# A pass over eight graphs laid out anew: two woven parts and one more graph in flight

## The chip, the cores and the metric

The kernel runs on one core of one Trainium2 chip. The metric is the device time of one execution in microseconds, taken as the median over several runs. The profile is one further execution, recorded by the hardware profiler.

## What is computed

Eight graphs of 1024 nodes with 128 features each go through two layers, each a graph step and an expert step, every one on the normed residual stream and added to it.

```python
# layer 0, graph step: maximum over the first 25 neighbours by number
feats = jnp.where(valid[..., None], x[idx], -inf);  agg = feats.max(axis=2)
x = x + relu(concat([norm(x), agg]) @ W + b)
# layer 0, experts: 8 experts 128 -> 512 -> 128 (exact gelu), best two of each row
x = x + sum_e w_dense[:, e] * (gelu(norm(x) @ W1[e] + b1[e]) @ W2[e] + b2[e])
# layer 1, graph step: attention, 8 heads of 16, masked by the adjacency matrix
scores = where(adj > 0, q @ k.T / 4, -1e9);  x = x + softmax(scores) @ v @ Wo + bo
# layer 1, experts: 6 experts of three 128 x 128 layers, best two of each row
```

## The kernel before

**Order.** All engines walk one list of steps per pass, made in Python by `schedule` and `weave`. Each engine runs its own share of every step, in the list's order, and waits on semaphores where another engine or a DMA is needed. So an engine that waits holds up all that stands behind it in the list. DMAs are issued by SP (waits in order too) and by POOL, which issues the indirect ones.

**Pass.** A full pass does four things for four graphs: attention and second expert layer of graph b (flag `att`), first expert layer of b+1 (`unit`), graph step and routing of b+2 (`near`), loading and norming of b+3 (`load`). There are 11 passes, b = -3 to 7; five of them (0 to 4) are full.

**First stage** of a full pass. For 8 row tiles and 8 heads the step `s` computes 128 x 1024 scores (two bf16 matmuls, line 1521, into one of two PA banks) and VectorE adds the mask and takes the row maximum (line 1193). Woven in are the 23 blocks of the first expert layer: weights of a block loaded into one of three slots of `wbuf` (`wl`), up (line 1494), gelu on ScalarE (line 1323), down (line 1506). Two searches for neighbours (`find`) and their gathers (line 791) come between, too.

**Second stage.** Score products again in transposed form with mask and maximum inside the matmul (`st`, lines 1544 and 1547), exponential on ScalarE (line 1340), value products (`av`, line 1559), normalization (`fin`) and output projection (`proj`), 4 groups of 8 steps. Between them the other searches (`find` 2 to 7), gathers, slot maxima (`pmax`, lines 924 to 931), and at its start the fetch of the sorted expert rows (line 833) and their addition (`comb`, line 1041).

**Third stage.** Norm of the attention result (`lnv` 3, `ln` 3), transposes and router (`t1`, `r1`, `lg1`), then the 12 expert steps of the second expert layer (`u1`, `u2`, `y1`, `acc1`; lines 1601, 1608, 1616, 1091). Spread over them lies a chain: the graph step of b+2 (`gT`, `gnn`), norms, query, key and value of b+1 (`qT`, `qk`, `v`), routing of b+2 (`lg0`, `cha` 0, `rank`), dispatch of its rows (`disp`, line 823), norm of b+3. Query and key are split into three bf16 parts, stored to `parts_dram` and loaded as stacks into QS and KS.

## Time and profile before

| | us |
|---|---|
| median of 3 runs | 3739.25 (3731.97 to 3746.79) |
| profiled execution, its own time | 3723.76 |
| its span in the trace | 3721.9 |
| busy: TensorE, VectorE, ScalarE, GpSimd | 2235.3, 1751.5, 1199.4, 1129.4 |

PE is TensorE, DVE VectorE, ACT ScalarE, POOL GpSimd. Busy time is that in which an instruction of the engine runs; the profile gives idle time and what ended it apart. The granted clock is the share of TensorE's full clock; 0.50 is its lower level of 1.2 GHz, 1.00 the upper of 2.4 GHz. Time and span differ by 1.9 us, and the median stands 15.5 us above the profiled execution.

### The profile page before, as it was taken

How to read it: one execution, taken by the hardware profiler on the slowest of the kernel's cores; microseconds unless marked ns; L12 is line 12 of the kernel's file. 1: busy time of each engine (PE TensorE's matmuls, PEld its weight loads, DVE VectorE, ACT ScalarE, POOL GpSimd, SP SyncE). 2: the span in 40 equal slices, each digit the busy share in tenths (PEclk: the TensorE clock that was granted, in tenths of full speed). 3: DMA queues.
4: the chain of work that ended last, by engine and by line, in shares of the span. 5: the costliest groups of instructions: out<-in, count | busy, mean ns of one | idle time of the engine just before them, and what ended most of it. 6: DMA issues, size and time to landing. Idle time of an engine off the chain costs nothing.

```text
span 3721.9 us, 46486 instructions
## 1 busy us (share of the span) xinstructions
PE 2235.3 (60%) x14209; PEld 1335.1 (36%) x14209; DVE 1751.5 (47%) x5158; ACT 1199.4 (32%) x2272; POOL 1129.4 (30%) x1245
## 2 busy tenths in 40 slices
PE   0013214677656766677656766677567757896687
PEld 0013212443425333443335333443335433643044
DVE  4223116652565336652565336652575437614813
ACT  0002111235313442235322433235223532363044
POOL 3535451425132431425132431424133431010000
PEclk9986655789868877789868877788768977997588
DMA  4425635633356325633357225734257325502200
GB/s 94 49 31 141 102 67 107 165 88 48 54 141 158 45 37 104 165 92 48 53 142 160 42 38 108 162 96 47 38 144 175 47 35 114 168 9 43 59 1 7
DMA packets 190540, 318.62 MB, mean 86 GB/s; under 512 B 28832, under 2 KB 115101, under 8 KB 190237
## 3 DMA queue, kind: packets, MB, share of 16 engines
q1 hardware_dynamic: 149788, 221.18, 22.3%
q0 software_dynamic: 40448, 93.92, 18.8%
q8 instruction: 126, 2.06, 0.2%
q14 instruction: 178, 1.45, 0.1%
HBM read 271.67 MB, written 42.93 MB: 85 GB/s over the span
## 4 chain that ended last, share of the span: by engine, by line
issue 26%; PE 23%; DVE 22%; DMA 17%; POOL 4%; DVEq 4%; ACT 2%; SPq 2%; POOLq 1%; ACTq 0%
DMA wbuf<-in_L_ffn_W 9%; DVE parts L1193 7%; PE PH L1494 4%; DMA parts_dram<-parts 3%; PE PY L1506 3%; POOL G L791 3%; DMA xn<-in_x 3%; PE PA L1544 2%; PE PY L1559 2%; PE PA L1547 2%; PE PA L1521 2%; DVE G L924 2%; DVEq L845 1%; DVE xn L874 1%; POOL rows_cols L833 1%
## 5 line engine op out<-in xcount | busy, mean ns | idle before, releaser
L791 POOL DMA_INDIRECT G<-table,slot_idx x792 | 814.8, 1029 | 379.9 <-issue 379.9
L1193 DVE CUSTOM_DVE_ANT_0 parts<-PA,mask 128x1024 bf16<-128x1024 f32 x512 | 626.2, 1223 | 250.4 <-issue 250.4
L1340 ACT ACTIVATE HB<-PA 128x1024 f32<-128x1024 f32 x512 | 497.4, 1019 | 496.1 <-PE PA L1547 495.9
L1521 PE MATMUL PA<-KS,QS 96*128 96x512 bf16 x1024 | 405.1, 491 | 224.0 <-DVE MX L1193 174.3
L1544 PE MATMUL PA<-QS,KS 99*128 99x512 bf16 x1024 | 412.1, 402 | 85.4 <-ACT HB L1340 48.9
L631 POOL TENSOR_TENSOR pool_pad<-pool_pad 1x1 f32<-1x1 f32 x128 | 28.6, 224 | 1424.5 <-DVE expert L1032 553.3
L1547 PE MATMUL PA<-identb,mask 128*128 128x128 bf16 x4096 | 414.4, 225 | 0.0
L1494 PE MATMUL PH<-rows_cols,wbuf 128*128 128x128 f32 x1472 | 254.2, 328 | 242.3 <-DMA wbuf<-in_L_ffn_W 193.4
L1547 PEld LDWEIGHTS PA<-identb,mask 128*128 128x128 bf16 x4096 | 331.6, 101 | 135.3 <-issue 21.7
L1323 ACT ACTIVATE HB<-PH,wbuf 128x128 f32<-128x128 f32 x736 | 209.6, 368 | 453.9 <-PE PH L1494 451.1
L634 DVE MEMSET dve_pad<- 1x1 f32 x686 | 40.4, 59 | 635.2 <-DMA G<-table,slot_idx 362.9
L1494 PEld LDWEIGHTS PH<-rows_cols,wbuf 128*128 128x128 f32 x1472 | 224.8, 232 | 302.9 <-DMA wbuf<-in_L_ffn_W 200.8
L1559 PE MATMUL PY<-HB,VS 128*32 128x512 f32 x2048 | 282.0, 624 | 7.1 <-ACT HB L1340 7.1
L1521 PEld LDWEIGHTS PA<-KS,QS 96*128 96x128 bf16 x1024 | 89.9, 108 | 414.0 <-DVE MX L1193 347.8
L1506 PEld LDWEIGHTS PY<-wbuf,HB 128*128 128x128 f32 x1472 | 226.2, 224 | 26.0 <-issue 7.4
L1506 PE MATMUL PY<-wbuf,HB 128*128 128x128 f32 x1472 | 230.2, 308 | 0.7 <-ACT HB L1323 0.7
L1370 PE MATMUL PH<-ident,xn 128*128 128x128 f32 x320 | 64.0, 352 | 249.3 <-DVE xn L874 94.1
L1544 PEld LDWEIGHTS PA<-QS,KS 99*128 99x128 bf16 x1024 | 102.7, 100 | 262.1 <-ACT HB L1340 170.3
L1359 ACT ACTIVATE HB<-PH,bias_T 128x512 f32<-128x512 f32 x192 | 131.5, 686 | 193.7 <-PE PH L1601 130.6
L1263 ACT ACTIVATE edges<-adj_sb 128x1024 uint8<-128x1024 int32 x64 | 67.8, 1060 | 385.3 <-DMA adj_sb<-in_adj 385.1
L1388 PE MATMUL PH<-excess,ones 128*1 128x2 f32 x128 | 12.2, 165 | 271.6 <-ACT excess L1266 231.5
L1616 PE MATMUL PY<-ew_sb,HB 128*128 128x128 f32 x768 | 122.5, 311 | 66.0 <-DVE mask L1091 62.3
(197 smaller groups left out, 2808.0 us busy)
## 6 DMA issues: line engine op xcount, KB each, us to landing
wbuf<-in_L_ffn_W SPq DMA_DIRECT2D x184, 514.0 KB, 4.9
adjm<-in_adj SPq DMA_DIRECT2D x64, 512.0 KB
adj_sb<-in_adj POOLq DMA_DIRECT2D x48, 512.0 KB, 3.9
G<-table,slot_idx POOLq DMA_INDIRECT x792
parts_dram<-parts SPq DMA_DIRECT2D x16, 768.0 KB, 6.8
QS<-parts_dram SPq DMA_DIRECT2D x48, 256.0 KB, 8.4
KS<-parts_dram SPq DMA_DIRECT2D x48, 256.0 KB, 8.4
rows_cols<-sorted_x SPq DMA_DIRECT2D x40, 256.0 KB, 4.7
```

The lines of the kernel that those rows point to most:

```text
L791: pool.indirect_dma_start(G[:, t % 2, s, :], None, table, bass.IndirectOffsetOnAxis(slot_idx[:, t, s:s + 1], axis=0), bounds_check=ROWS - ...
L1193: ins = dve.tensor_tensor_reduce(out=junk, in0=psum(ps, step)[:, :], in1=mask[:, t, :], scale=1.0, scalar=LOWEST, op0=ALU.add, op1=ALU.max ...
L1323: ins = act.activation(HB[:, 1, j % 2, c * P:(c + 1) * P], psum(ps, step)[:, c * P:(c + 1) * P], ACT.Gelu, bias=wbuf[:, j % WRING, 2 * HID ...
L1340: act.activation(HB[:, kc % 2, 2 * pr:2 * pr + 2, :], psum(ps, key)[:, :].rearrange("p (h q) -> p h q", h=2), ACT.Exp, scale=float(D) ** - ...
L1359: act.activation(HB[:, 0, k + j % 2, :], psum(ps, step)[:, :], ACT.Relu, bias=bias_T[:, col + e:col + e + 1]).then_inc(*emptied(ps, step))
L1494: ins = pe.matmul(psum(ps, step)[:, c * P:(c + 1) * P], wbuf[:, j % WRING, c * P:(c + 1) * P], cols_x[:, g % 2, q * P:(q + 1) * P], start= ...
L1506: ins = pe.matmul(psum(ps, ("y", g))[:, q * C:(q + 1) * C], HB[:, 1, j % 2, c * P:(c + 1) * P], wbuf[:, j % WRING, HID0 + c * C:HID0 + (c ...
L1521: ins = pe.matmul(psum(ps, step)[:, half[hf]], QS[0:SROWS, h, t * P:(t + 1) * P], KS[0:SROWS, h, half[hf]], start=True, stop=True)
L1544: pe.matmul(o, KS[0:SROWS + PARTS, h, kc * P:(kc + 1) * P], QS[0:SROWS + PARTS, h, half[qh]], start=True, stop=False)
L1547: ins = pe.matmul(o[:, qt * P:(qt + 1) * P], mask[:, qh * HTILES + qt, kc * P:(kc + 1) * P], identb[:, :], start=False, stop=(qt == HTILES ...
L1559: ins = pe.matmul(psum(ps, key)[32 * hh:32 * hh + 32, :], VS[:, kc, (D + 1) * (g * GH + hh):(D + 1) * (g * GH + hh) + 32], HB[:, kc % 2, h ...
L1616: ins = pe.matmul(psum(ps, step)[:, tt * C:(tt + 1) * C], HB[:, 0, 2 + j % 2, tt * P:(tt + 1) * P], ew_sb[:, 2, e, :], start=True, stop=True)
```

## The change

The pass becomes two parts, A and B, each an order merged from streams by planned times (`merge`): the step with the earliest planned time goes next, unless a step that it must follow, or the one that frees its PSUM bank, isn't placed yet. The planned times only order the list; nothing waits for them.

Part A (planned times 0 to 130): the second expert layer of graph b-1 with its norm and router; score maxima of b; expert blocks of b+1; `pmax` 3 to 7 of b+2 with the fetches of tiles 4 to 7. Part B (0 to 118): value products of b; graph step, norm, routing and dispatch of b+2; fetch and joining of expert rows, norm, query and key of b+1; load, norm, table, all eight searches, four fetches and three `pmax` of b+3. Then `stack`, `v`, the last `fin` and `proj`.

A fifth flag, `late`, stands for the second expert layer of b-1. There are 12 passes, b = -3 to 8; four of them (1 to 4) are full. The stage of the last expert layer runs alone in the last pass.

Further: weights of the blocks have six slots (four in `wbuf`, one in HB, one in `parts`) in place of three; their biases come no longer with the weights but are worked out by VectorE after `rank` (`block_b1`). Gathered slots beyond the eighth go to one shared buffer `G_more`, so their fetch waits for `pmax` t-1. The stacks of QS and KS are loaded after the last `st` in a step of their own. All adjacency loads come from SP. `gT`, `gnn`, `r1`, `lg0`, `lg1`, `rank`, `chb` and `chc` take banks PH; `y1` takes PA. Four residual buffers stand where there were two and a piece of the mask; norms have their own small tiles.

```diff
-FINDS_EARLY = 10
 BLOCKS = 2 * TILES + E0 - 1
 PER_GROUP = 4
 GROUPS = (BLOCKS + PER_GROUP - 1) // PER_GROUP
-WRING = 3
-BLOCKS_FROM = 22.0
-WCOLS = 2 * HID0 + HC
+WOWN = 4
+WRING = WOWN + 2
+WCOLS = 2 * HID0
+FETCHED = 4
+POOLED = FETCHED - 1
...
+def merge(streams, held):
+    s, done = [], set()
+    heads = [0] * len(streams)
+    known = {step for stream in streams for _, step, _ in stream}
+    while any(h < len(stream) for h, stream in zip(heads, streams)):
+        best = None
+        for n, stream in enumerate(streams):
+            if heads[n] == len(stream):
+                continue
+            when, step, after = stream[heads[n]]
+            if any(a in known and a not in done for a in after) or best and best[0] <= when:
+                continue
+            taken = {name: list(held[name]) for name in held}
+            for name, key, _ in signals(step):
+                if name in BANKS:
+                    if len(taken[name]) >= BANKS[name]:
+                        before = taken[name][-BANKS[name]]
+                        if before in known and before not in done and before != step:
+                            break
+                    taken[name].append(empties(step, key))
+            else:
+                best = when, n, step, taken
+        _, n, step, taken = best
+        heads[n] += 1
+        done.add(step)
+        for name in held:
+            held[name][:] = taken[name][-4:]
         s.append(step)
+    return s
+def over(begin, end, steps):
+    return [(begin + (end - begin) * n / len(steps), step, after) for n, (step, after) in enumerate(steps)]
+def chained(times, steps):
+    return [(t, step, (steps[n - 1],) if n else ()) for n, (t, step) in enumerate(zip(times, steps))]
...
+def schedule(late, att, unit, near, load):
+    n1 = len(ORDER1)
+    streams = []
+    tail = []
+    if late:
+        tail += [("x2",)]
+    if att or unit:
+        tail += [("take",)]
+    if near:
+        tail += [("load_res",)]
+    streams.append([(0.0, k, ()) for k in tail])
+    if late:
+        streams.append(chained((0, 4, 11, 15, 20, 20.1, 28, 31),
+                               [("lnv", 3), ("ln", 3), ("t1",), ("r1",), ("lg1",), ("cha", 1), ("chb", 1), ("chc", 1)]))
+        experts = []
+        for k in range(n1 + 2):
+            if k < n1:
+                experts.append((("u1", k), (("t1",),)))
+            if 1 <= k <= n1:
+                experts.append((("u2", k - 1), (("u1", k - 1),)))
+            if k >= 2:
+                experts.append((("y1", k - 2), (("u2", k - 2),)))
+                experts.append((("acc1", k - 2), (("y1", k - 2), ("chc", 1))))
+        streams.append(over(33, 128, experts) + [(128.0, ("store",), ())])
+    if near:
+        streams.append([(15.0 * (t - POOLED), ("pmax", t), (("fetch", t),)) for t in range(POOLED, TILES)])
+        streams.append([(15.0 * (t - POOLED) - 14.0, ("fetch", t), (("pmax", t - 1),)) for t in range(FETCHED, TILES)])
     if att:
+        scores = []
         for t in range(TILES):
+            scores.append((("mask", t), (("load_mask", t),)))
+            for h in range(HEADS):
+                scores.append((("s", t, h), ()))
+                if h == 2 and t + 1 < TILES:
+                    scores.append((("load_mask", t + 1), (("mask", t),)))
+        streams.append(over(9, 130, scores))
     if unit:
+        first = [("xs", 0), ("xs", 1)] + [("wl", j) for j in range(WRING)]
+        blocks = [(("xT", 0), (("xs", 0),))]
         for j in range(BLOCKS + 1):
             if j < BLOCKS:
                 if j % PER_GROUP == 2 and j // PER_GROUP + 1 < GROUPS:
+                    g = j // PER_GROUP + 1
+                    blocks.append((("xT", g), (("xs", g),)))
+                    if g + 1 < GROUPS:
+                        blocks.append((("xs", g + 1), ()))
+                blocks.append((("up", j), ()))
             if j > 0:
+                blocks.append((("dn", j - 1), ()))
                 if j - 1 + WRING < BLOCKS:
+                    blocks.append((("wl", j - 1 + WRING), ()))
                 g, last = group_of(j - 1)
                 if last:
+                    blocks += [(("yc", g), ()), (("yst", g), ())]
+        streams.append([(0.0, k, ()) for k in first] + over(7, 116, blocks))
+    held = {"A": [], "H": [], "Y": []}
+    s = merge([k for k in streams if k], held)
+    streams = [[(0.0, ("shift",), ())]]
     if att:
+        streams.append(chained((0.1, 1.5), [("mparts",), ("mT",)]))
+        values = []
+        groups = [(qh, g) for qh in range(2) for g in range(2)]
         for n, (qh, g) in enumerate(groups):
             for kc in range(TILES):
+                values.append((("st", qh, g, kc), (("mT",),)))
                 if kc == 1 and n > 0:
+                    values.append((("fin", *groups[n - 1]), ()))
                 if kc == 3 and n == 2:
+                    values.append((("proj", 0), ()))
                 if kc > 0:
+                    values.append((("av", qh, g, kc - 1), ()))
+            values.append((("av", qh, g, TILES - 1), ()))
+        streams.append(over(5, 118, values))
+    if near:
+        graphs = chained((0.2, 5, 5.1, 12, 17, 23, 27, 27.1),
+                         [("gT",), ("gnn",), ("gnn_add",), ("lnv", 1), ("ln", 1), ("t0",), ("lg0",), ("cha", 0)])
+        if not unit:
+            graphs.insert(1, (0.3, ("bias",), ()))
+        graphs += [(47.0, ("rank",), (("comb",),)), (54.0, ("disp",), ()),
+                   (56.0, ("chb", 0), (("comb",),)), (57.0, ("chc", 0), ())]
+        streams.append(graphs)
+    if unit:
+        streams.append([(2.0, ("fetch_y",), ())])
+        streams.append([(36.0, ("comb",), (("fetch_y",),)), (38.0, ("lnv", 2), ()), (43.0, ("ln", 2), ()),
+                        (50.0, ("qT",), (("lg0",),)), (57.0, ("qk", 0), ()), (67.0, ("qk", 1), ()),
+                        (75.0, ("next_mask",), ())])
+    if load:
+        streams.append([(7.0, ("load_x",), (("gT",),)), (19.0, ("lnv", 0), ()), (23.0, ("ln", 0), ()),
+                        (28.0, ("store_x",), ())])
+        finds = [(8.0, ("load_adj", 0), ()), (8.0, ("load_adj", 1), ()),
+                 (9.0, ("deg", 0), (("gT",),)), (11.0, ("class", 0), ())]
+        for t in range(TILES):
+            when = 14.0 + 12.5 * t
+            finds.append((when, ("find", t), ()))
+            if t + 2 < TILES:
+                finds.append((when + 2, ("load_adj", t + 2), ()))
+            if t + 1 < TILES:
+                finds.append((when + 5, ("deg", t + 1), ()))
+                finds.append((when + 9, ("class", t + 1), ()))
+        streams.append(finds)
+        streams.append([(30.0 + 15.0 * t, ("fetch", t), (("find", t), ("store_x",), ("pmax", t - 1)))
+                        for t in range(FETCHED)])
+        streams.append([(82.0 + 17.0 * t, ("pmax", t), (("fetch", t),)) for t in range(POOLED)])
+    s += merge([k for k in streams if k], held)
+    if unit:
+        s += [("stack",), ("v",)]
     if att:
...
+    if k == "fetch":
+        t = step[1]
+        return [(f"gat{t % 2}", step, 16 * SLOTS)]
...
-        return Y(*step)
+        return A(*step)
...
-        wbuf = sb("wbuf", [P, WRING, WCOLS])
+        wbuf = sb("wbuf", [P, WOWN, WCOLS])
...
-        G = sb("G", [P, 2, SLOTS, C])
+        G = sb("G", [P, 2, CLASS_SLOTS[0], C])
+        G_more = sb("G_more", [P, SLOTS - CLASS_SLOTS[0], C])
...
+        XF = XT2
         rest = tmp
-        CT = tmp
-        ctxn = xn[:, 0:HTILES, :]
+        col_sums = WT
+        wslots = [wbuf[:, i, :] for i in range(WOWN)]
...
-            parts_of = (g >= 0, 0 <= g + 1 < GRAPHS, 0 <= g + 2 < GRAPHS, g + 3 < GRAPHS)
-            if g > 0 and all(parts_of):
+        for g in range(-3, GRAPHS + 1):
+            parts_of = tuple(0 <= g + ahead < GRAPHS for ahead in (-1, 0, 1, 2, 3))
+            if g > 1 and all(parts_of):
                 continue
             passes.append((g, Pass(state, *parts_of)))
-            loops = GRAPHS - 3 if all(parts_of) else 1
...
-                        for j, k in enumerate(which):
+                    elif kind == "stack":
+                        sp.wait_ge(*at(ps, turn, "pd", ("qk", 1)))
+                        if ps.att:
+                            sp.sem_inc(s_slot, 1)
+                            sp.wait_ge(*is_full(ps, turn, ("st", 1, 1, TILES - 1, 1)))
+                        stacks = [(i, stack, j, k) for i, (stack, which) in enumerate(((QS, QPART), (KS, KPART)))
+                                  for j, k in enumerate(which)]
+                        for n, (i, stack, j, k) in enumerate(stacks):
+                            if ps.att and n == len(stacks) - 1:
+                                sp.wait_ge(*is_full(ps, turn, ("av", 1, 1)))
                             sp.dma_start(stack[D * j:D * j + D, :, :],
...
+                    for s in range(few - 2, few):
+                        fetch(s)
+                    if t >= 1:
+                        pool.wait_ge(*at(ps, turn, "aggr", ("pmax", t - 1)))
+                        held_by(pool, pool_pad, True)
...
+                settle(dve.tensor_scalar(expert_f[:, :], expert_f[:, :], float(E0 - 1), None, ALU.min))
+                dve.tensor_copy(expert[:, :], expert_f[0:1, :]).then_inc(S["pos"], 1)
+                settle(dve.tensor_tensor(passed[:, :, :], expert_f[:, :].unsqueeze(2).to_broadcast([P, BLOCKS, EP]),
+                                         eidx[:, 0:1, :].to_broadcast([P, BLOCKS, EP]), ALU.is_equal))
+                for lo, hi in ((0, BLOCKS // 2), (BLOCKS // 2, BLOCKS)):
+                    n = hi - lo
+                    spare = tmp[:, 0:n * HC * EP].rearrange("p (j c e) -> p j c e", c=HC, e=EP)
+                    settle(dve.tensor_tensor(spare, passed[:, lo:hi, :].unsqueeze(2).to_broadcast([P, n, HC, EP]),
+                                             b1_sb[:, :, :].unsqueeze(1).to_broadcast([P, n, HC, EP]), ALU.mult))
+                    settle(dve.tensor_reduce(out=block_b1[:, lo:hi, :], in_=spare, axis=AX.X, op=ALU.add))
...
+                        if j == 0:
+                            act.wait_ge(*at(ps, turn, "bb"))
...
```

## Rows read from the trace of the kernel before

**Rows 1.** The page: the span, and the busy time of each engine.
```profile
span 3721.9 us, 46486 instructions
...
PE 2235.3 (60%) x14209; PEld 1335.1 (36%) x14209; DVE 1751.5 (47%) x5158; ACT 1199.4 (32%) x2272; POOL 1129.4 (30%) x1245
```

**Rows 2.** Line 1193 in five windows: duration min/median/max, first and last start.
```profile
L1193 DVE CUSTOM_DVE_ANT_0 parts<-PA,mask x64: 1218/1224/1226, 636.5 to 788.2; 128x1024 bf16<-128x1024 f32 x64
...
L1193 DVE CUSTOM_DVE_ANT_0 parts<-PA,mask x64: 1218/1224/1226, 1475.0 to 1627.9; 128x1024 bf16<-128x1024 f32 x64
...
L1193 DVE CUSTOM_DVE_ANT_0 parts<-PA,mask x64: 1218/1223/1225, 2737.0 to 2885.2; 128x1024 bf16<-128x1024 f32 x64
...
L1193 DVE CUSTOM_DVE_ANT_0 parts<-PA,mask x64: 1218/1224/1226, 3132.5 to 3238.2; 128x1024 bf16<-128x1024 f32 x64
...
L1193 DVE CUSTOM_DVE_ANT_0 parts<-PA,mask x64: 1223/1224/1225, 3453.2 to 3547.5; 128x1024 bf16<-128x1024 f32 x64
```

**Rows 3.** Windows: length; busy of PE, PEld, DVE, ACT, POOL; clock; DMA share; GB/s.
```profile
1475.00:1629.00 154.00, 102.70 (x522) 70.43 (x521) 102.25 (x224) 39.89 (x123) 43.43 (x46) 0.75 0.59 147
1629.00:1786.00 157.00, 107.84 (x949) 56.54 (x949) 50.29 (x129) 73.94 (x102) 77.96 (x87) 0.83 0.29 44
1786.00:1895.00 109.00, 70.10 (x306) 42.78 (x306) 64.98 (x290) 35.57 (x59) 17.23 (x18) 0.80 0.46 90
3132.00:3240.00 108.00, 88.23 (x499) 58.38 (x500) 87.70 (x204) 32.72 (x100) 7.21 (x8) 0.84 0.60 181
3453.00:3549.00 96.00, 64.16 (x124) 8.16 (x124) 87.80 (x203) 0.00 (x0) 0.00 (x0) 0.50 0.12 39
3549.00:3662.00 113.00, 100.40 (x939) 52.21 (x939) 9.95 (x25) 64.60 (x67) 0.00 (x0) 0.95 0.01 2
3662.00:3722.00 60.00, 42.01 (x177) 24.95 (x177) 25.68 (x121) 20.99 (x32) 0.00 (x0) 0.81 0.03 10
```

**Rows 4.** The same for two short windows.
```profile
1490.00:1510.00 20.00, 6.21 (x12) 0.79 (x12) 17.50 (x33) 0.00 (x0) 0.18 (x1) 0.50 0.33 110
1730.00:1750.00 20.00, 18.20 (x181) 9.55 (x179) 5.79 (x15) 14.13 (x22) 9.76 (x12) 1.00 0.28 54
```

**Rows 5.** Lines, 1475 to 1629 us: count, busy, mean ns, idle before and releaser.
```profile
L791 POOL DMA_INDIRECT G<-table,slot_idx x41 | 41.7, 1017 | 13.3 <-issue 13.3
L1494 PE MATMUL PH<-rows_cols,wbuf 128*128 128x128 f32 x184 | 34.8, 350 | 28.5 <-DMA wbuf<-in_L_ffn_W 27.4 <-ACT rows_cols L1317 0.9
```

**Rows 6.** Waits, 1629 to 1786 us: total, times, longest.
```profile
PE PH L1569 <- DVE tmp L1222: 29.0, 3, 19.0
...
DVE res_n L1041 <- issue: 19.9, 1, 19.9
...
DVE dve_pad L634 <- DMA G<-table,slot_idx: 18.0, 2, 12.9
```

**Rows 7.** Lines of the whole span, gathers, scatters, slot maxima and table loads.
```profile
L791 POOL DMA_INDIRECT G<-table,slot_idx x792 | 814.8, 1029 | 379.9 <-issue 379.9
...
L833 POOL DMA_INDIRECT rows_cols<-sorted_y,place x128 | 127.8, 998 | 56.8 <-issue 56.8
L823 POOL DMA_INDIRECT sorted_x<-xn,place x128 | 125.2, 978 | 49.5 <-issue 49.5
...
L924 DVE TENSOR_TENSOR G<-G 128x256 f32<-128x256 f32 (+5 forms) x154 | 110.9, 720 | 59.7 <-issue 53.0
...
L1278 ACT ACT_TABLE_LOAD x24 | 30.8, 1283 | 23.9 <-DVE sd L859 23.5
...
L1107 DVE TENSOR_TENSOR parts<-tmp,parts 128x512 bf16<-128x512 f32 x32 | 22.1, 692 | 2.4
```

**Rows 8.** DMA issues: count, size of one, median us to landing.
```profile
wbuf<-in_L_ffn_W SPq DMA_DIRECT2D x184, 514.0 KB, 4.9
...
QS<-parts_dram SPq DMA_DIRECT2D x48, 256.0 KB, 8.4
```

**Rows 9.** Line 791 in 1629 to 1786 us, as in group 5.
```profile
L791 POOL DMA_INDIRECT G<-table,slot_idx x55 | 56.8, 1033 | 32.6 <-issue 32.6
```

384 lines of the change are left out of this document (132 added, 252 removed).

## Prediction

> **What bounds the kernel now.** I read the share of busy time first: TensorE works 2235 of 3722 us, VectorE 1752 [rows 1]. No engine fills the span, so the limits change from stage to stage or come from waits. The score line at different places shows the beat: first scores at 636.5 us, then from 1475.0 to 2737.0 three passes, 420.7 us each; the pass from 3132.5 to 3453.2 takes 321 us, and 269 us follow to the end [rows 1, 2]. The windows split a full pass into 154 us of scores with blocks and two searches, 157 us of values with six searches and 109 us of second expert layer with the chain [rows 3]. In the first DVE is busy 102 of 154 us with PE at 103, in the second PE 108 of 157 with DVE at 50, in the third PE 70 and DVE 65 of 109. Each stage leaves room on both.
>
> The last passes show the same stages with less beside them, and these are the best prices in the trace. Scores alone: 96 us, limited by DVE, which is busy 87.8; a stretch full of scores has DVE at 17.5 of 20 us, its practical top, and PE at 6 with the clock at 0.50 [rows 3, 4]. Scores and blocks without searches and gathers: 108 us, with PE 88 and DMA at 181 GB/s. Values alone: 113 us, PE busy 100 at clock 0.95. Second expert layer alone, from the norm to the store: 60 us, PE 42, DVE 26 [rows 3].
>
> **Part A** puts scores, blocks, second expert layer and five slot maxima together. On DVE: scores with masks 96 us; expert layer 25.7 busy, at 17.5 of 20 some 29 us; slot maxima 110.9 us at their main line over 64 tiles [rows 7], 1.7 us each, with final step and waits between dependent steps about 3, so five cost 15; copies of the residual 2. Sum 142 us. On PE: 88 for scores and blocks and 42 for the expert layer make 130 busy; the fullest stretch has 18.2 of 20 [rows 4], so 143 us. DMA: 181 GB/s over 108 us are 19.5 MB; the gathers of four tiles add 38 x 64 KB, result and residual 1 MB, together 23 MB or 127 us at that rate. Three loads near 140 us have to interlock. The stage with scores and blocks took 108 us against 96 on DVE, a factor of 1.13. The one with two searches took 154 against 96 and two searches of about 11 us, a factor of 1.31; there the blocks waited 27.4 us for weights [rows 5], with three slots, and gathers shared the DMA engines. Six slots should take much of that wait away, but four tiles of gathers remain. I take 1.18, so 167 us, between 142 and 1.31 x 142 = 186.
>
> At the seam the stacks come late. They are 12 loads of 256 KB, one landing after 8.4 us [rows 8]; 3.1 MB at 181 GB/s are 17 us from the last `st`. The last `av`, `fin`, `proj` and the copies hide about 12, and SP stands at the stack and then at `load_res`, so the first six weight loads follow behind. I add 5 us to each A, between 0 and 15: A = 172.
>
> **Part B** puts values and the chain together. On PE: 100 busy for the values; the third stage's 70 less the layer's 42 leave 28 for the chain; 128 busy, at the 100.4 of 113 that the values reach alone 144 us. If the 49 us of PE's idle time in the present value stage stayed, it would be 177. Part of that idle time had a cause that the plan addresses: PE waited 29.0 us in three `fin` steps for the copy by DVE, which itself stood 19.9 us for the joined expert rows and 18.0 for gathers [rows 6]. `comb` is now planned at 36, after 20 us of fetch. On DVE the searches and the rest are the pass's 217 us of busy time less about 128 in A, so some 90, or 103 at its top density; not the limit. The new block biases are four passes over 384 elements of a row; the nearest row is 128 x 512 at 0.69 us [rows 7], so at most 2.8 us, and `rank`'s other readers go first.
>
> POOL decides more. A gather costs 1.51 us with its idle time (814.8 + 379.9 over 792), a fetch of expert rows 1.44 and a scatter 1.36 [rows 7]. In B it does 16 fetches (23 us), then tile 0 once the new table is stored (about 35), 25 gathers (38 us, to 73), the dispatch (22, to 95), tile 1 (16 gathers, to 119), tile 2 (about 10, to 134). 41 gathers for two tiles are read from the first stage [rows 5]; the other six tiles share 58. Then `pmax` 2 can run at about 140 where 116 is planned, and DVE, PE and the rest behind it in the list wait for it. About 15 us of values and the 12 us of `fin` and `proj` follow. B = 165, between 144 and 190.
>
> A full pass is thus 337 us in place of 421. ScalarE is at 74 of 157 us in the value stage and 40 of 154 in the first, so it hides its new work. A norm's square root between exponentials or gelus costs table loads; they are 1.28 us each and there are 24 at the norm line now, three per full pass [rows 7]. I count four more per pass, 5 us, hidden. The Trainium skill, in "ScalarE: Activation LUTs", What ACT_TABLE_LOAD costs, speaks against such mixing: every switch of set costs the load and a drain, some 2.66 us, and calls should be batched by set. By it the four would cost 11 us per pass; as an estimate 80 us over the kernel if nothing hid them. The rows agree on the 1283 ns of the load; the drain they do not show.
>
> **The sum.** Before its first scores the kernel still has to gather for two graphs and run the blocks of one. The two woven parts bring these together, but one chain on POOL remains; I take 615 us for 636.5, between 560 and 670. b = 0 has no second expert layer: on DVE 113 us, at 1.18 with the seam 140, and 165: 305. Four full passes: 4 x 337 = 1348. b = 5, without searches: 172 + 150. b = 6, without graph work: 160 + 130. b = 7: scores and expert layer, 125 us on DVE, so 137, and 113 for values. b = 8: 60. Together 615 + 305 + 1348 + 322 + 290 + 250 + 60 = 3190; 1.9 us lie around the span and the median stood 15.5 above the profiled execution: **3207 us**, with 3100 to 3320 if A and B stay within 10 us each of these values.
>
> **The rivals.** *POOL and DMA keep the beat* (0.27). With A and B shorter, gathers and weight loads meet more often. If tiles 0 to 3 take more gathers, or `G_more` with its wait for `pmax` t-1 stops POOL at tile 1, B becomes 185; if gathers slow the weights as in the first stage now, A 186. The pass takes 371 us, and six such passes give 3207 + 6 x 34 = 3410. For it speak the 154 us against 108 [rows 3]. A gather took 1.34 us with its idle time in the first stage, 1.63 in the second [rows 5, 9], though the latter waits for tiles between. The Trainium skill, "SBUF — State Buffer", says that a two-port VectorE operation locks GpSimd out of writing descriptors; that would be one cause. A busier DVE would then lengthen the gathers, and the rows so far do not show it, since the stage with more DVE work has the cheaper ones.
>
> *Everything fits* (0.08). The clock rises with fuller PE, A comes to 150 and B to 150: 3207 - 6 x 37 = 2990.
>
> *The order stalls the engines, slower than before* (0.12). Engines run one written order, by planned times that sum to 248 us where I expect 337. B has about 20 places at which PE waits for DVE or ScalarE in a chain step (`fin`, `proj`, `t0`, `lg0`, `rank`, `qT`, `class` and so on), while DVE may itself wait for a gather. Three such places cost 29.0 us before, about 10 each [rows 6]. If all 20 cost 5 us more than I allow, a pass grows by 100 us and the time is 3207 + 6 x 100 = 3810. The change is slower from 90 us per pass, 4.5 us a place. Against it: the steps of a stream stand several values apart, and values alone leave ScalarE and DVE enough time to answer.
>
> *Most of the gain is lost* (0.05): the same with half the price, or weaving that hides little, 3500 to 3720.
>
> **How the numbers follow.** The forecast has 0.48. The range is 3030 to 3500: it takes the forecast's own, POOL's case, and the upper part of the good one. About 0.5% is what a measurement of this kernel can tell from no change. Faster by more 0.87, within it 0.02, slower by more 0.11.
>
> **What would show it.** First scores from pass to pass every 337 us; A near 172 with DVE over 75% busy and a mean clock above the 0.75 of the first stage; little waiting of PE for wbuf; in B POOL in work nearly throughout until `pmax` 2, and DVE's waits before slot maxima 1 and 2. Wrong would be: B over 200 with PE waiting at chain steps; weight waits as long as now; a long pause between the last `st` and the first scores.

## The result and the profile after

The changed kernel takes 3597.73 us (3594.47 to 3601.75), the kernel before on the same chip 3735.61 (3727.08 to 3746.79): a ratio of 0.963, interval 0.960 to 0.966. The direction was as forecast. The size was not: 138 us gained where 3207 us stood for 532, and the time lies above the upper end of the range, 3500. The profiled execution took 3601.75 us.

The head of the page of after, its span and its busy times, answers to [rows 1]:

```profile
span 3599.6 us, 46254 instructions
...
PE 2146.0 (60%) x14209; PEld 1346.9 (37%) x14209; DVE 1776.8 (49%) x5239; ACT 1226.7 (34%) x2295; POOL 1106.3 (31%) x1215
```

TensorE has 89 us less work, VectorE 25 us more, and the span is 122 us shorter. TensorE still fills 60% of it, VectorE 49% instead of 47: no engine is near to filling it.

The score line in six windows answers to [rows 2]. It is line 1221 now; each line gives the first and the last of 64 maxima of one graph (its custom instruction alone; the shortest, the median and the longest in ns ahead of the times):

```profile
L1221 DVE CUSTOM_DVE_ANT_0 parts<-PA,mask x64: 1218/1224/1226, 720.8 to 851.3; 128x1024 bf16<-128x1024 f32 x64
...
L1221 DVE CUSTOM_DVE_ANT_0 parts<-PA,mask x64: 1218/1220/1225, 1460.3 to 1626.2; 128x1024 bf16<-128x1024 f32 x64
...
L1221 DVE CUSTOM_DVE_ANT_0 parts<-PA,mask x64: 1218/1220/1225, 1848.1 to 2017.5; 128x1024 bf16<-128x1024 f32 x64
...
L1221 DVE CUSTOM_DVE_ANT_0 parts<-PA,mask x64: 1218/1220/1225, 2640.9 to 2810.3; 128x1024 bf16<-128x1024 f32 x64
...
L1221 DVE CUSTOM_DVE_ANT_0 parts<-PA,mask x64: 1216/1220/1225, 2977.5 to 3127.5; 128x1024 bf16<-128x1024 f32 x64
...
L1221 DVE CUSTOM_DVE_ANT_0 parts<-PA,mask x64: 1214/1220/1226, 3279.1 to 3421.0; 128x1024 bf16<-128x1024 f32 x64
```

First scores at 720.8 instead of 636.5 us: the beginning became longer, not shorter. Then 1460.3 to 1848.1, one full pass, is 388 us instead of 420.7, and 1848.1 to 2640.9, two more, are 396 each. The passes after that take 337 and 302 us, as the work beside the scores goes away.

For the windows I cut each pass at two steps that are easy to find in the trace: A begins where the residual of the graph is kept (step `x2`) and ends where the maxima leave for the value stage (step `mparts`); B goes from there to the next `x2`. The columns are window, length, busy us of PE, weight load, DVE, ACT and POOL with their counts, granted clock, DMA share, GB/s. The rows are A and B of b = 2, A and B of b = 7, and the last expert layer alone; they answer to [rows 3]:

```profile
1444.20:1628.00 183.80, 137.37 (x708) 96.94 (x708) 121.08 (x348) 57.00 (x140) 49.71 (x54) 0.82 0.47 125
1628.00:1831.70 203.70, 130.11 (x1070) 72.81 (x1068) 97.94 (x301) 97.18 (x148) 88.35 (x93) 0.80 0.46 80
3261.00:3423.00 162.00, 95.29 (x305) 42.22 (x305) 112.24 (x322) 20.99 (x32) 0.00 (x0) 0.74 0.18 38
3423.00:3534.00 111.00, 100.06 (x939) 51.96 (x939) 8.53 (x22) 64.43 (x67) 0.00 (x0) 0.96 0.01 2
3534.00:3600.00 66.00, 44.07 (x178) 26.19 (x177) 27.29 (x124) 21.09 (x33) 0.00 (x0) 0.79 0.03 9
```

| part | predicted | measured |
|---|---|---|
| up to the first scores | 615 | 721 |
| b = 0, A and B | 140 + 165 = 305 | 133 + 199 = 332 |
| A of b = 1 to 4 | 172 | 187, 185, 188, 219 |
| B of b = 1 to 4 | 165 | 204, 203, 187, 181 |
| b = 5 | 172 + 150 | 206 + 141 |
| b = 6 | 160 + 130 | 176 + 131 |
| b = 7 | 137 + 113 | 163 + 113 |
| b = 8 | 60 | 64 |

The differences are 106 + 27 + 206 (four full passes) + 25 + 17 + 25 + 4 = 410 us, the whole distance from 3190 to the span of 3600. Added up by kind of part, the beginning is 106 us too long, the B's are 140 (34 in b = 0, 39, 38, 22 and 16 in the full passes) and the A's 160 (91 in the full passes, half of it in b = 4, and 34, 16 and 26 in b = 5 to 7).

**B of b = 2.** Its waits, 1628 to 1832 us (engine, operand and line, what ended the wait, us in total, times, longest):

```profile
POOL pool_pad L636 <- DMA table<-xn: 43.9, 1, 43.9
DVE dve_pad L639 <- DMA G_more<-table,slot_idx: 42.0, 2, 31.4
...
PE PH L1604 <- DVE rows_y L1255: 35.1, 1, 35.1
```

The work itself is where I put it: PE is busy 130 of 204 us where I summed 128, DVE 98 where I took some 90. But DVE waits 42 us for gathered slots beyond the eighth, and PE 35 us in the last `fin`, which waits for DVE. The time line of the end of tiles 1 and 2 shows how (start in us, length, engine, instruction; in brackets the idle time ahead of it and what ended it):

```profile
1774.95 0.06 DVE L639 MEMSET dve_pad<- 1x1 f32 x1 [10.62 <-DMA G_more<-table,slot_idx]
...
1775.37 0.18 POOL L636 TENSOR_TENSOR pool_pad<-pool_pad 1x1 f32<-1x1 f32 x1 [5.15 <-issue]
1775.93 1.23 DVE L941 TENSOR_TENSOR G<-G,G_more 128x1024 f32<-128x1024 f32 x1 [0.92 <-issue]
...
1776.96 1.08 POOL L803 DMA_INDIRECT G<-table,slot_idx  x1 [1.40 <-issue]
...
1779.15 0.06 DVE L956 MEMSET dve_pad<- 1x1 f32 x1 [0.29 <-issue]
...
1787.73 0.18 POOL L636 TENSOR_TENSOR pool_pad<-pool_pad 1x1 f32<-1x1 f32 x1
1799.83 1.01 POOL L803 DMA_INDIRECT G_more<-table,slot_idx  x1 [11.91 <-issue]
...
1808.95 0.99 POOL L803 DMA_INDIRECT G_more<-table,slot_idx  x1 [0.30 <-issue]
...
1814.94 0.06 DVE L639 MEMSET dve_pad<- 1x1 f32 x1 [31.37 <-DMA G_more<-table,slot_idx]
```

DVE gets tile 1's extra slots at 1774.95 and is done with them at 1779.15 (line 956 is the signal). GpSimd issues eight gathers of tile 2 up to 1787.7, stands 11.9 us, issues eight more into `G_more` from 1799.8 to 1809, and they have landed at 1814.94. That is 187 us into B where I put slot maximum 2 at about 140. The value products had been through at 1783.1, 155 us into B, and 17 us follow on slot maximum 2 to the end of B. At tile 1 the buffer was in use: GpSimd went on right after slot maximum 0. In B of b = 3 and 4 tile 2 has eight slots and tile 3 sixteen; these B's are shorter, and the A's behind them begin with a longer wait.

**A of b = 2.** Its longest waits of PE (1444 to 1628 us):

```profile
PE PA L1556 <- DVE res_f L1115: 20.1, 9, 3.6
...
PE PH L1519 <- DMA rows_cols<-sorted_x: 14.0, 1, 14.0
...
PE PH L1529 <- DMA wbuf<-in_L_ffn_W: 2.5, 2, 1.5
```

Waits for block weights are down to 2.5 us from 27.4 [rows 5]. Three steps take their place. The blocks' rows, dispatched at the end of B, arrive 14 us late. The second expert layer's product `y1` now uses bank PA, which the scores use, so that PE waits 20.1 us for the addition by DVE (line 1115, `acc1`), nine times. And the scores begin 17 us after the start of `x2`.

### The profile page after: what moved, and what is told of

It is laid out like the page before. It is cut to its first block, busy times and chain, and to the rows that moved or that the text cites. A ratio compares the mean times of both kernels' runs of the same rounds, so it can differ in the third digit from the quotient of the medians.

```text
span 3599.6 us, 46254 instructions
## 1 busy us (share of the span) xinstructions
PE 2146.0 (60%) x14209; PEld 1346.9 (37%) x14209; DVE 1776.8 (49%) x5239; ACT 1226.7 (34%) x2295; POOL 1106.3 (31%) x1215
## 4 chain that ended last, share of the span: by engine, by line
issue 35%; DVE 27%; PE 26%; DVEq 5%; ACT 4%; DMA 2%; SPq 1%; ACTq 0%
DVE parts L1221 7%; PE PA L1579 4%; PE PA L1582 4%; PE PY L1594 4%; ACT HB L1375 2%; PE PH L1529 2%; DVEq L861 2%; DVE res_f L1115 2%; PE PA L1556 2%; PE PY L1541 2%; DVE score L909 1%; DVE top L913 1%; PE PH L1636 1%; DMA rows_cols<-sorted_x 1%; DVE st L870 1%
## 5 line engine op out<-in xcount | busy, mean ns | idle before, releaser
L803 POOL DMA_INDIRECT G<-table,slot_idx x512 | 526.7, 1029 | 270.2 <-issue 270.2
L1556 PE MATMUL PA<-KS,QS 96*128 96x512 bf16 x1024 | 356.2, 441 | 261.5 <-DVE res_f L1115 141.5
L803 POOL DMA_INDIRECT G_more<-table,slot_idx x280 | 287.1, 1025 | 173.4 <-issue 173.4
L1358 ACT ACTIVATE HB<-PH,block_b 128x128 f32<-128x128 f32 x736 | 209.6, 368 | 353.7 <-PE PH L1529 353.6
L1519 PE MATMUL PH<-ident,rows_cols 128*128 128x128 f32 x184 | 35.4, 323 | 264.7 <-DMA rows_cols<-sorted_x 264.7
L1529 PE MATMUL PH<-rows_cols,wbuf 128*128 128x128 f32 x1024 | 166.8, 317 | 28.1 <-DMA wbuf<-in_L_ffn_W 20.0
L1529 PEld LDWEIGHTS PH<-rows_cols,wbuf 128*128 128x128 f32 x1024 | 158.5, 230 | 61.7 <-issue 29.0
L1285 ACT ACTIVATE XT<-PH 128x512 f32<-128x512 f32 x96 | 54.5, 597 | 358.6 <-PE PH L1405 358.3
L839 POOL DMA_INDIRECT sorted_x<-xn,place x128 | 130.6, 1020 | 65.2 <-issue 65.2
L1541 PEld LDWEIGHTS PY<-wbuf,HB 128*128 128x128 f32 x1024 | 142.3, 206 | 21.7 <-issue 10.9
```

What stands on the lines that cost most here:

```text
L803: pool.indirect_dma_start(G[:, t % 2, s, :] if s < few else G_more[:, s - few, :], None, table, bass.IndirectOffsetOnAxis(slot_idx[:, t, s ...
L839: pool.indirect_dma_start(sorted_x, bass.IndirectOffsetOnAxis(place[:, j:j + 1], axis=0), xn[:, j % TILES, :], None, bounds_check=BLOCKS * ...
L1358: ins = act.activation(HB[:, 1, j % 2, c * P:(c + 1) * P], psum(ps, step)[:, c * P:(c + 1) * P], ACT.Gelu, bias=block_b1[:, j, c:c + 1])
L1529: ins = pe.matmul(psum(ps, step)[:, c * P:(c + 1) * P], wslots[j % WRING][:, c * P:(c + 1) * P], cols_x[:, g % 2, q * P:(q + 1) * P], star ...
L1541: ins = pe.matmul(psum(ps, ("y", g))[:, q * C:(q + 1) * C], HB[:, 1, j % 2, c * P:(c + 1) * P], wslots[j % WRING][:, HID0 + c * C:HID0 + ( ...
L1556: ins = pe.matmul(psum(ps, step)[:, half[hf]], QS[0:SROWS, h, t * P:(t + 1) * P], KS[0:SROWS, h, half[hf]], start=True, stop=True)
```

## The experiments

Five chips were used, called here the first to the fifth. Each kernel is compared with the kernel before on its own chip. Lengths of parts are compared across the first two, where the kernel before takes 3732 and 3724 us; the change itself was not run on the second. On the first chip ran the change itself again, eight slots, the split stacks and three weight slots:

> The changed kernel itself, unaltered, as a measure for the variants on the chip on which they run. On the first chip its ratio to the kernel before was 0.963. If the other chip only stretches all work alike, the ratio is 0.96 again; if it adds waits of its own to the longer chains of the two parts, it is nearer to 1, about 0.98.

Measured: 3593.04 us against 3731.71, ratio 0.9625 (0.9587 to 0.9662).

### Eight slots only

```diff
-                which = pool.value_load(degree_class[0:1, t:t + 1], ...)
...
-                with pool.If(which < 1):
-                    fetch(few - 2, ...); fetch(few - 1, ...)
+                fetch(few - 2, ...); fetch(few - 1, ...)
+                return
```

> Gathers and slot maxima are cut to eight slots for every tile (tiles with more neighbours are left incomplete): 64 gathers per graph for 97, none into G_more, so no wait for the buffer that tiles share. Theory 1, gathers through one queue and one shared buffer set the end of B: VectorE's two waits in B of 10.6 and 31.4 us fall under 5 us each, B from 204 to about 170, and the first three passes, which are nothing but this chain, shrink by 50 us or more: about 0.065 of the time, ratio to before near 0.90. Theory 2, chain steps of TensorE set B: B stays over 190, the ratio at 0.95 or above.

Measured: 3218.43 us, ratio 0.862 (0.8585 to 0.8654). The score line and the windows of A and B of b = 2:

```profile
L1213 DVE CUSTOM_DVE_ANT_0 parts<-PA,mask x64: 1220/1225/1226, 534.8 to 659.7; 128x1024 bf16<-128x1024 f32 x64
...
L1213 DVE CUSTOM_DVE_ANT_0 parts<-PA,mask x64: 1219/1220/1225, 1206.1 to 1363.2; 128x1024 bf16<-128x1024 f32 x64
...
L1213 DVE CUSTOM_DVE_ANT_0 parts<-PA,mask x64: 1219/1220/1226, 1560.4 to 1717.5; 128x1024 bf16<-128x1024 f32 x64
```

```profile
1186.20:1365.00 178.80, 130.95 (x708) 91.62 (x709) 121.28 (x350) 57.04 (x140) 40.34 (x45) 0.84 0.51 131
1365.00:1540.00 175.00, 127.58 (x1070) 71.22 (x1068) 92.48 (x298) 97.21 (x148) 61.81 (x67) 0.85 0.34 78
```

The first scores come at 535 us and B falls from 203 to 175; A is 179 instead of 185. GpSimd is busy 62 us in B instead of 88. So the slots beyond the eighth cost 375 us of the kernel; I had expected a ratio of 0.90, not 0.862. Of these 186 lie before the first scores and 43 in b = 0, since 721 and 332 us became 535 and 289. In the full passes 140 us go, 85 in the B's and 41 in A of b = 4, and what is left over my 165 is 9 to 12 us in three B's and nothing in the fourth. That the whole kernel comes to my 3207 plus 11 is chance in part: 80 us less than I had before the first scores stand against 67 more in the four full passes. The edit takes the slots' transfers, DVE's maxima over them and the shared buffer away together; two of the next runs take it apart in part.

### Two buffers for the extra slots

```diff
-        G_more = sb("G_more", [P, SLOTS - CLASS_SLOTS[0], C])
+        G_more = sb("G_more", [P, 2, SLOTS - CLASS_SLOTS[0], C])
...
-                    if t >= 1:
-                        pool.wait_ge(*at(ps, turn, "aggr", ("pmax", t - 1)))
-                        held_by(pool, pool_pad, True)
```

The room comes from the ring of weights (`WOWN` 1 instead of 4). In the order a fetch no longer follows slot maximum t-1 but t-2, and by that the dispatch comes to stand behind tile 1's gathers instead of ahead of them.

> All 97 gathers stay, but the slots beyond the eighth get a buffer for even and one for odd tiles, so that they wait for the slot maximum of tile t-2 and not of tile t-1. The room comes from the weights: one slot of their own in place of four, three in all, which the run with three slots showed to cost nothing. It tells the two halves of the gather theory apart, the number of gathers (33 more than in the run with eight slots, 1.5 us each, 50 us per graph) and the wait for the shared buffer. If the shared buffer is the cost: VectorE's wait of 31.4 us at the end of B falls under 8 us, B from 204 to about 178, the first three passes lose 60 us or more; together near 3400, ratio 0.91. If the number of gathers is the cost: B stays over 195, ratio 0.955 or above.

Measured on the second chip: 3507.24 us against 3724.39, ratio 0.9423 (0.9399 to 0.9447); the change stood at 0.9625 on the first. B of b = 2 falls from 203 to 192, first scores from 721 to 702, A is 188. Tile 2 on GpSimd now:

```profile
1733.62 1.04 POOL L803 DMA_INDIRECT G<-table,slot_idx  x1 [1.42 <-issue]
...
1743.56 1.00 POOL L803 DMA_INDIRECT G<-table,slot_idx  x1 [0.30 <-issue]
...
1744.86 0.99 POOL L803 DMA_INDIRECT G_more<-table,slot_idx  x1 [0.30 <-issue]
...
1753.96 0.99 POOL L803 DMA_INDIRECT G_more<-table,slot_idx  x1 [0.30 <-issue]
1754.97 0.18 POOL L636 TENSOR_TENSOR pool_pad<-pool_pad 1x1 f32<-1x1 f32 x1
...
1767.46 0.18 POOL L636 TENSOR_TENSOR pool_pad<-pool_pad 1x1 f32<-1x1 f32 x1 [12.31 <-issue]
```

Sixteen gathers in a row take 21 us, where the change needed 33, and the pause is gone. At tile 2 it had not been the buffer that was in use: in after slot maximum 1 had ended at 1779.15, before the pause began. What stands there is `held_by` (line 636), an addition of one element with a drain behind it. Where this pair follows at once on gathers, GpSimd's next instruction comes late, here 12.31 us after sixteen gathers, in after 5.15 and 11.91 us. DVE still waits for tile 2:

```profile
DVE dve_pad L639 <- DMA G_more<-table,slot_idx: 28.9, 1, 28.9
```

The B's of the full passes are 10, 11, 10 and 14 us shorter. In b = 2 only 5 of the 11 us are tile 2's own: from its first gather until DVE has it pass 33 us instead of 38, though the issues take 12 less. Without the pause the last gather lands 12.8 us after its issue (1753.96 to 1766.71) instead of 6 (1808.95 to 1814.94), so more than half of the pause was time that tile 2's transfers needed anyway. The other 6 us are a start 142 instead of 149 us into B, by the shorter wait at tile 1 and the moved dispatch, which no run takes apart. The ratio lies between my two cases, 0.91 and 0.955. The larger rest is the work that stands ahead of slot maximum 2 in GpSimd's queue, from which the next run moves the slot maximum away.

### Fewer tiles fetched in B

```diff
-FETCHED = 4
+FETCHED = 3
```

> FETCHED 3 on the chip of the unaltered kernel: three fetches and two slot maxima in B, five and six in A. With the run of eight slots, B without the chain is 175 us. Only the wait for tile 2, 31.4 us, leaves B, A takes up a slot maximum and may wait for tile 2's gathers at its start. Gather theory: B 178, A up by 5 to 15, ratio to before 0.93 to 0.945. If the wait only moves over the seam: 0.96.

Measured: 3534.68 us, ratio 0.9474 (0.9444 to 0.9504), on the second chip too. The fetch of tile 3 and slot maximum 2 are now in A. B of b = 2 is 175 (minus 28), the same as with eight slots. But A grows from 185 to 208, and the scores of its graph start 27 us after `x2` instead of 17. Of the 28 us that the order takes out of B, 23 come back behind the seam. The rest of the gain is in the first scores (706) and in b = 0 (297 instead of 332).

### `y1` in the banks PH

```diff
-        return A(*step)
+        return H(*step)
```

> y1 in a bank of PH, on the chip of the unaltered kernel. If sharing PA is the cost: TensorE's wait of 20 us for VectorE's adding of experts goes and A falls by 10 to 20 us, ratio 0.925 to 0.945. If VectorE sets A, or the PH banks stop the blocks: 0.955 to 0.97.

Measured on the second chip: 3545.25 us, ratio 0.9518 (0.9495 to 0.954). A of b = 2 is 180 instead of 185. In b = 7, where only scores and the expert layer stand, the score line runs

```profile
L1221 DVE CUSTOM_DVE_ANT_0 parts<-PA,mask x64: 1214/1224/1225, 3235.6 to 3359.2; 128x1024 bf16<-128x1024 f32 x64
```

from 3235.6 to 3359.2 us: 124 us against 142 in after (3279.1 to 3421.0), and that is the 125 us that I had worked out for VectorE alone. So the shared bank lengthens A by 5 to 12 us in the full passes and by 18 in b = 7, 68 us over b = 1 to 7, which the prediction had left out. The last expert layer alone gets 7 us longer with it (71 instead of 64). The gain is less than the 0.925 to 0.945 that I had expected.

### The stacks in two steps

```diff
-                            sp.dma_start(stack[D * j:D * j + D, :, :],
-                                         parts_v[i, k, :, :, :])...
+                            sp.dma_start(stack[D * j:D * j + D, lo:lo + GH, :],
+                                         parts_v[i, k, :, lo:lo + GH, :])...
+        streams.append([(91.0, ("stack0",), (("qk", 1), ("st", 1, 0, TILES - 1)))])
```

Four of the eight heads' stacks are loaded as soon as the last `st` of these heads is done.

> Heads 0 to 3 of QS and KS, which the last group of value products no longer reads, are loaded after the last st of group (1,0), some 30 us earlier; heads 4 to 7 stay where they are. Theory, the seam: in part A the first scores wait for the stacks (16.9 us from the kept residual to the first score in the changed kernel, 19.7 us of TensorE's wait in the last scores), and the weights and sorted rows queue behind 3.1 MB. With half of it gone the first rows land 8 us earlier: 6 to 10 us in each of seven seams, 40 to 70 us, 0.015 of the time. Rival: the loads meet gathers of tiles 1 and 2, on which VectorE waits at that time, and B grows by as much: no difference over 0.5%.

Measured on the first chip: 3547.76 us, ratio 0.9516 (0.9479 to 0.9554), 45 us less than the change on this chip. In b = 7 the first scores stand 8 us after `x2` instead of 19:

```profile
L1223 DVE CUSTOM_DVE_ANT_0 parts<-PA,mask x64: 1219/1224/1225, 3225.0 to 3363.4; 128x1024 bf16<-128x1024 f32 x64
```

A falls by 15 us each in b = 6 and 7, whose seams were 24 and 19 us. In the full passes the seam gives 1 us: something else is late there, among it the dispatched rows. The rest of the 45 us is 1 to 7 us in many parts, the most of it before the first scores and in A of b = 0; two profiles of the change differ by up to 5 us in a part.

### Three weight slots

```diff
-WRING = WOWN + 2
+WRING = 3
```

> Three weight slots in place of six, everything else as in the changed kernel. TensorE waits 2.5 us for weights in a part A of the changed kernel, 27.4 us in the first stage of the kernel before. Theory, the deeper ring is what took that wait away: it returns in part, 10 to 25 us in each of seven passes with blocks, 70 to 170 us, ratio to before 0.98 to 1.01. Rival, the looser order of A gives each block so much time that three slots are enough: ratio within 0.5% of the unaltered kernel.

Measured on the first chip: 3584.50 us, ratio 0.9604 (0.9565 to 0.9644), not to be told from the change. PE's wait for weights in A of b = 2 is 1.8 us against 2.5. What took the 27.4 us of [rows 5] away is therefore not the number of slots. The blocks are spread over 184 us in place of 154 with their weights ahead of them in the order; which of these does it was not tried.

### Together

Two buffers, `y1` in PH and the split stacks in one kernel:

> The three changes together: own buffers for the slots of even and odd tiles with three weight slots, stacks loaded in two halves, y1 in PH. If the three act on different places (end of B, seam, inside of A), the gains add: from 0.9625 some 0.05, 0.011 and 0.025, ratio near 0.875, 3270 us. If one wait hides behind another, it comes to 0.90 to 0.92.

Measured on the second chip: 3426.05 us against 3724.39, ratio 0.9203 (0.9188 to 0.9218): faster than both kernels, than the change by 4.4% by the two ratios. The three edits alone gave 0.020, 0.011 and 0.011 against the change, together 0.042, and this is the 0.042 between 0.9625 and 0.9203: the gains add. I had expected 0.875 in that case because I had set the single gains too high. The windows of A and B of b = 2:

```profile
1389.50:1564.00 174.50, 132.64 (x712) 92.74 (x712) 122.34 (x350) 57.77 (x142) 46.27 (x53) 0.85 0.49 130
1564.00:1755.30 191.30, 129.03 (x1064) 72.03 (x1064) 98.17 (x302) 96.47 (x147) 91.34 (x93) 0.83 0.46 86
```

A fell from 185 to 175 and B from 203 to 191; first scores at 700.

Then with three tiles fetched in B (best2), with a late dispatch on top (best3), and the eight-slot kernel with `y1` in PH and the split stacks (eight_all), on the third chip:

> The three changes (two buffers for slots beyond the eighth, split stacks, y1 in PH) with FETCHED 3, so that tile 2's slot maximum and tile 3's fetch move into part A. If the order of the queue is the cost, B loses the 29.9 us wait and A gains under 12: ratio 0.89 to 0.90, from 0.9203. If GpSimd's work as such is the cost, the wait shows up in A: 0.915 to 0.925.

> As the one before, and the dispatch behind the third fetch in place of behind the first. With own buffers nothing else stops GpSimd at tile 1, so its gathers and tile 2's end 30 us earlier, and the dispatch has the rest of B for itself. Order theory: a further 5 to 15 us per pass, ratio 0.875 to 0.89. Rival: sorted rows are then late for the blocks of the next part A, and the ratio is that of the run before or worse.

> Eight slots only (tiles with more neighbours are left incomplete), one buffer as in the changed kernel, six weight slots, stacks split, y1 in PH. B stays at 175 less 5. A was 179 with eight slots: if shared banks and seam are what lies above my 142 us of VectorE work, A falls to 155 and the ratio from 0.862 to about 0.82. If the mutual waits of the woven order are the cost, A stays over 168, ratio 0.84 to 0.85.

The kernel before takes 3939.81 us there, these 3774.70 (ratio 0.9565, 0.9527 to 0.9603), 3780.26 (0.9586, 0.9548 to 0.9624) and 3390.45 (0.860, 0.8559 to 0.864). With three tiles fetched in B the late dispatch changes nothing that can be measured. In eight_all A of the full passes is 174 to 180 us with a seam of 14, and the A's of b = 1 to 7 are together 87 us shorter than with eight slots alone on the first chip, 30 of them in b = 7. So the two other edits do show. But B of the full passes takes 213 to 219 where it took 164 to 177, and the ratio is the one that eight slots alone had. These B's belong to the chip, as the last runs show for the change; eight slots alone did not run here.

### The other chips

Four single edits ran on the fourth chip. The first of them:

```diff
-        graphs += [..., (54.0, ("disp",), ()), ...]
+        streams.append([(117.5, ("disp",), (("rank",), ("fetch", FETCHED - 1)))])
```

> Only the place of the dispatch in the order changes: in part B it comes behind the fourth fetch (planned 117.5) in place of behind the first (54). Theory 1, the one queue of GpSimd sets the end of B: in the profile of the changed kernel VectorE stands 10.6 and 31.4 us before the slot maxima of tiles 1 and 2, while the dispatch with its wait took GpSimd from 1707 to 1743 us. Without it ahead, the gathers of tiles 1 and 2 end 36 us earlier, VectorE's waits for them fall from 42 to under 12 us per pass, and B from 204 to about 172; in the six passes that fetch, about 180 us: 3420 us. Theory 2, B is limited by the chain steps that TensorE waits for and the gather wait only lies in front of them: B stays over 195 and the time over 3560. Theory 3, the dispatch then ends so late that part A waits for its sorted rows: B falls, A grows by as much.

> FETCHED 3 in place of 4: part B does three fetches and two slot maxima, part A five fetches and six slot maxima. Theory 1 (GpSimd's queue sets the end of B): the wait of 31.4 us for tile 2 leaves B, B falls from 204 to about 175, A grows by 3 us of slot maximum and by what it waits for tile 2's gathers at its start, at most 10: the time is about 3460. Theory 2 (chain steps limit B): B over 195, time over 3560. A rival on A's side: the wait of VectorE only moves behind the seam, A grows by as much as B loses, 3590.

> FETCHED 2: part B does two fetches and one slot maximum, part A six fetches and seven slot maxima. Theory 1: both waits, 42 us, leave B; B is near 165 as its TensorE work of 130 us at 0.9 busy allows with its start; A grows by two slot maxima of 3 us, and its gathers (56 of 97) meet the weight loads: A 187 to 200. The time is about 3430 if A hides them, 3520 if GpSimd's 85 us of gathers in A stop VectorE. Theory 2: over 3560.

> The last matmuls of an expert of layer 1 (y1) take a bank of PH in place of PA. In part A of the changed kernel TensorE waits 20.1 us for VectorE's adding of experts (line 1115), which frees the PA bank that the next score needs. Theory 1, sharing PA is the cost: the wait goes, part A falls from 185 by 10 to 20 us, the seven parts A with this layer give 70 to 140 us: 3460 to 3530. Rival: the PH banks, now held until VectorE has added, stop the blocks' up products; part A stays or grows, 3600 to 3700. Second rival: VectorE and its many waits for the next score set A whatever bank is used: within 1% of 3598.

| edit | us | ratio | A (seam) of b = 2 | B of b = 2 | first scores |
|---|---|---|---|---|---|
| dispatch behind the fetches | 3900.08 | 0.9899 (0.9866 to 0.9932) | 213 (33) | 233 | 727 |
| three tiles in B | 3854.49 | 0.9774 (0.9729 to 0.9819) | 201 (22) | 242 | 706 |
| two tiles in B | 3873.75 | 0.9826 (0.9785 to 0.9866) | 210 (14) | 242 | 673 |
| `y1` in PH | 3834.48 | 0.9735 (0.9692 to 0.9777) | 182 (18) | 257 | 716 |

The kernel before took 3947.70 us here. Against the kernel with `y1` moved the late dispatch has a B 24 us shorter and an A 31 us longer, 15 of them in the seam; some 5 to 12 of the 31 are the gain of the moved `y1`. It is the same trade over the seam. It could not bring tiles 1 and 2 forward by the 36 us that I expected, because the shared buffer holds tile 1: with the dispatch gone GpSimd stands there in B of b = 2 until slot maximum 0,

```profile
POOL pool_pad L637 <- DVE dve_pad L957: 60.0, 1, 60.0
```

which DVE reaches in its own order. Two tiles move the first scores 33 us forward against three, but A of b = 0 to 2 is 20, 13 and 9 us longer, and the kernel is 19 us slower.

These B are 30 to 54 us longer than the change's on the first chip. Three runs on the fifth chip, where the kernel before takes 3902.03 us, ask whether that belongs to the edits:

> The changed kernel unaltered. On the chip with 3730 us: 0.9625. On the other: FETCHED 3 alone gave 0.977 and y1 in PH alone 0.974 there, so 0.985 to 1.0 if these two gain as much there as on the first chip.

> best1 again, as a measure. On the chip with 3730 us for the kernel before: 0.92. On the chip with 3940 us, where B's chain steps wait more: 0.95 to 0.97, if the added waits fall into the chains that part B holds.

> Two buffers, split stacks, y1 in PH and FETCHED 3, beside best1 on the same chip. If the order of GpSimd's queue is the cost of the 29.9 us wait: 0.02 to 0.03 below best1. If GpSimd's work as such is the cost, the same as best1 within 0.005.

Measured: 3872.06 us (0.9918, 0.9888 to 0.9948), 3753.56 (0.9647, 0.9587 to 0.9708), 3742.82 (0.9598, 0.9541 to 0.9654). The unchanged change has A of 192 and 188 us for b = 1 and 2, about as before, and B of 252 and 253 instead of 204 and 203. It belongs to the chip. Three tiles or four cannot be told apart in the combined kernel, since the intervals overlap. Waits of the change here over the whole trace, which have no counterpart on the first chip:

```profile
ACT HB L1375 <- remote: 205.2, 52, 13.8
...
DVE WT L1095 <- remote: 89.7, 6, 17.7
...
ACT ed L1345 <- remote: 74.8, 5, 15.9
```

B of b = 2 on the fifth chip as a window, and two waits of GpSimd in it:

```profile
1732.40:1985.30 252.90, 143.81 (x1072) 77.48 (x1072) 98.19 (x301) 99.33 (x150) 84.67 (x93) 0.74 0.36 64
...
POOL pool_pad L636 <- DVE expert L1048: 32.8, 1, 32.8
POOL pool_pad L636 <- DVE dve_pad L956: 28.7, 1, 28.7
```

ACT stands 408 us in 87 such places and DVE 208 us in 26; "remote" says that the profile finds no instruction that ended just then. In 108 of the 113 the engine waits for a PSUM bank that PE fills: the signal comes later than the profile's end of the matmul. PE is busy 144 us in B of b = 2 (130 on the first chip), at a clock of 0.74 (0.80). GpSimd, too, waits for others there: 33 us for the routing (`rank`) and 29 for slot maximum 0, against 5.6 and 1.4 on the first chip. So on this chip its own queue is not all that sets B. What the change gains depends on the chip, 3.7% on the first and 0.8% on the fifth, and so does what the combined kernel gains, 8.0% and 3.5%.

## Why the prediction was right and wrong

**The work of the parts: right.** PE 130 us in B (128 summed), 137 in A (130); DVE is busy 121 in A where 142 was summed with its gaps. Without graph work the parts came out as worked out from the last passes: B of b = 6 131 us (130) and of b = 7 113 (113), B of b = 5 141 (150), the last layer 64 (60). The price of a stage from a place where it stands alone holds when it is moved.

**B = 165: wrong, the term of GpSimd's queue was mis-sized.** I had the chain and its order: tile 0, dispatch, tile 1, tile 2, slot maximum 2. In the trace tile 0's gathers begin 47.5 us into B (35), the dispatch ends at 109 (95), tile 1 at 142 (119), and tile 2 takes 16 gathers where I assumed ten, the last landing at 187 (140). The links are 12, 14, 23 and 47 us late. So the last alone adds 24: some 8 are the six more gathers, 7 pass between tile 1's last gather and tile 2's first, and 5 are the wait between its gathers, by the run with two buffers. I had tile 2's size from no row: the first stage shows 41 gathers for two tiles, and six others share the rest. Behind it PE's last `fin` waits 35 us. What follows on slot maximum 2 took 17 us, not the 27 that I had added. With eight slots B is 175, with two buffers 192, with slot maximum 2 and tile 3's fetch moved out 175: on the first two chips the runs bear out the chain and its price. On the fifth, where B is 253, the chain is held up from outside, by the 62 us that GpSimd waits for steps of DVE. The rival "POOL and DMA keep the beat" named this mechanism, down to `G_more` and its wait, but at 185 us; the measured first B's are 204 and 203, the later ones 187 and 181.

**The first scores at 615: wrong, and the largest miss of one row.** I argued that two woven parts bring the work together. But three of the slot maxima of the third graph now stand in the first B, ahead of all scores, and their 57 gathers at 1.51 us [rows 7] are 86 us that the kernel before had later. Of the 792 gathers 269 are issued before the first scores, where it had been 202. That was in the diff, `POOLED` 3, and in a row. With two tiles fetched in B the first scores come at 673, with eight slots at 535.

**A = 172: low by 13 to 16 us, and by 47 in b = 4.** The factor 1.18 was about right for the scores among blocks; what was left out is the bank shared by `y1` and the scores. It stands in the change's description and I gave it no price; the runs give 5 to 12 us in full passes and 18 in b = 7. The seam, 5 us allowed above its cover, was 15 to 17 us from b = 1 to 3 and 34 in b = 4 and 5. In b = 6 and 7 the stacks make it, 13 and 11 us less when split; in b = 2 PE waits 14 us for dispatched rows. In b = 4 and 5 DVE also stands 20 us for the extra slots of tile 3 at the start of A; with eight slots A of b = 4 is 178. Over all passes the A's miss by more than the B's, 160 us against 140.

**Weights: right that the wait goes, wrong on why.** With three slots it goes as well.

**ACT's table loads: right that they cost little, not that all are hidden.** Eleven per full pass instead of seven, 1283 ns each. The Trainium skill, in "ScalarE: Activation LUTs", What ACT_TABLE_LOAD costs, counts some 2.66 us for a switch of set; the four more per pass would be, as an estimate, 11 us by it. ACT is busy 57 us of 184 in A and 97 of 204 in B, and the longest waits of PE and DVE in both parts name other work. One in B of b = 2 does lie on PE's way: between two exponentials ACT waits 5.7 us for the norm's variance and then loads the table again, and PE stands 6.9 us.

```profile
1697.38 0.21 ACT L1311 ACTIVATE sq<-sd 128x8 f32<-128x8 f32 x1 [5.70 <-DVE sd L875]
...
1697.60 1.28 ACT L1375 ACT_TABLE_LOAD   x1
...
1699.98 0.61 PE L1579 MATMUL PA<-QS,KS 99*128 99x512 bf16 x1 [6.88 <-ACT HB L1375]
```

These traces have no record of a drain behind the load.

**The order stalling the engines, some 20 chain steps at 5 us each: did not happen on the first chip.** PE's largest wait in B is one of 35.1 us at the last `fin`, behind DVE's for gathers, and B without the extra slots leaves 10 us over my sum for all chain steps together. On the fifth chip B is 50 us longer, half of that rival's 100; that it is its mechanism is not shown. (In the sums of the rivals 3207 - 6 x 37 is 2985, not 2990.)

## What to carry to other kernels

When an order is rebuilt, write down for every engine that issues transfers the list of what it now issues in each part, with real counts per tile, and add up when the last one lands: the part cannot end earlier, whatever the other engines' sums say. A wait removed by moving its work over a seam mostly comes back on the other side, 23 of 28 us in one run here, 31 against 24 in another; what pays is less in the queue (no extra slots, 28 us a B) or a resource no longer shared (a PSUM bank, 5 to 12 us an A; two buffers with the order that they allow, 11 us a B). Price the beginning by the same list, since what is moved forward by one part runs there with nothing to hide it.

## What the runs showed of the chip

The same kernel took 3593 us on one chip and 3872 on another, the kernel before 3732 and 3902. The difference of the change sits in B, 204 against 252 us with an A of 185 to 192 on both, where ACT and DVE stand up to 17.7 us for banks whose matmuls the profile has as done. The granted clock over the span differs little, 0.801 and 0.786; in B of b = 2 it is 0.80 and 0.74, and whether that is cause or effect is not known. Why PE's signals come late there is open: no run took the stretches away.

A wait on GpSimd between gathers costs even when it has been met. Where the one-element addition with its drain followed at once on eight gathers, 3.3 to 13.9 us passed to the next instruction, half of the 62 cases under 5.1; after sixteen gathers, with two buffers, 6.2 to 14.0 in 18 cases. Where GpSimd had already stood for at least 1 us, it was 1.4 to 2.9. This points to something of the gathers that is still under way, and taking the pause out of tile 2 gave 5 us of its 12. No run varied the drain alone, so whether it waits for descriptors or for their landing stays open, as does whether some order of the gathers hides them; the orders tried moved the wait.
